# A two-layer transformer on one core: the low-rank factor split of layer 0's feed-forward moves from GpSimd to ScalarE and GpSimd together

## The reference, cut to what matters

```python
def _layernorm(x, axis=-1, eps=1e-05):
    m = jnp.mean(x, axis=axis, keepdims=True)
    v = jnp.var(x, axis=axis, keepdims=True)
    return (x - m) / jnp.sqrt(v + eps)

def _matmul_lora(x, w, a, b, scale=1.0):
    out = jnp.einsum('bsd,hd->bsh', x, w)
    out = out + jnp.einsum('bsr,hr->bsh', jnp.einsum('bsd,rd->bsr', x, a), b) * scale
    return out

mod = (_silu(L0_c) @ L0_wmod).reshape(L0_c.shape[0], 6, 1, -1)
sa, ca, ga, sb, cb, gb = (mod[:, 0], mod[:, 1], mod[:, 2], mod[:, 3], mod[:, 4], mod[:, 5])
...
h = _layernorm(x, axis=-1) * (1 + cb) + sb
gate = _matmul_lora(h, gate_w, gate_a, gate_b)          # x 1024x512, w 1376x512, a 16x512, b 1376x16
up = _matmul_lora(h, up_w, up_a, up_b)
out = _matmul_lora(silu(gate) * up, down_w, down_a, down_b)   # w 512x1376, a 16x1376, b 512x16
x = x + gb * out
```

## Time and profile before

| | before |
|---|---|
| median of three runs | 1750.19 us (1748.44 to 1757.35) |
| the profiled execution | 1748.17 us |
| its span, first to last instruction | 1746.3 us |
| mean granted TensorE clock over the span | 0.978 |
| PE busy | 1653.8 us (95%) |
| DVE busy | 1172.4 us (67%) |
| ACT busy | 1043.7 us (60%) |
| POOL busy | 746.5 us (43%) |

### The profile page before, as it was taken

One profiled execution on the slowest core, in us unless ns is written; L12 is line 12 of the kernel. 1 busy time (PEld: TensorE's weight loads), 2 busy tenths in 40 slices (PEclk: granted clock), 3 DMA queues, 4 the chain that ended last, 5 costly groups with the idle time before them and its releaser, 6 DMA issues. The chain is left out here.

```text
span 1746.3 us, 28528 instructions
## 1 busy us (share of the span) xinstructions
PE 1653.8 (95%) x10107; PEld 1338.6 (77%) x10123; DVE 1172.4 (67%) x2951; ACT 1043.7 (60%) x2261; POOL 746.5 (43%) x705
## 2 busy tenths in 40 slices
PE   4899999999999999999999699999988999999897
PEld 2689989999999989999988488878764555555476
DVE  5667677777777677777666843336777777776285
ACT  3477777877777777877777221114324666666553
POOL 3287585675856757567551300000352334321200
PEclk9999999999999999999999889999979999999998
DMA  6100100101011010000002312200230000000000
GB/s 195 38 14 22 28 25 19 32 13 38 13 31 25 20 37 13 25 19 26 13 19 79 101 40 69 67 2 19 84 82 14 1 1 1 1 1 1 1 19 31
DMA packets 75014, 55.82 MB, mean 32 GB/s; under 512 B 23502, under 2 KB 57998, under 8 KB 74874
## 3 DMA queue, kind: packets, MB, share of 16 engines
q1 hardware_dynamic: 73290, 53.21, 10.4%
q10 hardware_dynamic: 1584, 0.79, 0.2%
HBM read 51.88 MB, written 2.10 MB: 31 GB/s over the span
## 5 line engine op out<-in xcount | busy, mean ns | idle before, releaser
L792 PEld LDWEIGHTS psum<-a_probsT,a_v 128*128 128x128 f32 x2304 | 294.7, 191 | 25.6 <-issue 3.9
L792 PE MATMUL psum<-a_probsT,a_v 128*128 128x128 f32 x2304 | 299.2, 275 | 1.7 <-ACT a_probsT L1004 1.6
L893 DVE CUSTOM_DVE_ANT_0 psum<-psum,a_keys_allowed 128x128 f32<-128x128 f32 (+7 forms) x256 | 195.7, 764 | 83.0 <-PE psum L78 74.4
L2123 ACT ACTIVATE a_probsT<-psum 128x512 f32<-128x512 f32 (+1 forms) x304 | 168.4, 588 | 106.3 <-PE psum L1990 67.6
L987 ACT ACTIVATE a_probs<-psum,a_neg_max 128x128 f32<-128x128 f32 (+7 forms) x256 | 190.7, 745 | 66.6 <-DVE a_neg_max L893 58.2
L996 ACT ACTIVATE a_probs<-a_probs,a_row_inv 128x128 f32<-128x128 f32 (+7 forms) x256 | 201.1, 786 | 27.9 <-DVE a_row_inv L900 27.7
L649 POOL TENSOR_TENSOR a_turned_pool<-a_q_sum,a_sine 64x512 f32<-64x512 f32 x62 | 79.3, 1278 | 286.7 <-DVE a_q_sum L879 285.5
L923 DVE TENSOR_TENSOR a_ctxT_lo<-psum,a_ctxT_hi 128x128 fp32r<-128x128 f32 x256 | 73.7, 288 | 172.7 <-ACT a_ctxT_hi L1010 172.6
L1004 ACT COPY a_probsT<-psum 128x512 f32<-128x512 f32 (+3 forms) x384 | 173.2, 488 | 18.7 <-PE psum L780 16.6
L913 DVE SCALAR_TENSOR_TENSOR a_sumT<-psum,a_scale_o,a_sumT 128x512 f32<-128x512 f32 x248 | 173.6, 742 | 0.9 <-PE psum L806 0.7
L780 PE MATMUL psum<-ident,a_probs 128*128 128x128 f32 x1152 | 168.9, 274 | 0.5 <-ACT a_vT L981 0.3
(11 more groups left out here) (395 smaller groups left out, 3893.2 us busy)
## 6 DMA issues: line engine op xcount, KB each, us to landing
a_raw_o<-in_L_attn_qw_o SPq DMA_DIRECT2D x32, 256.0 KB, 2.8
a_raw_q<-in_L_attn_qw_q SPq DMA_DIRECT2D x31, 256.0 KB, 3.5
mod1b_w<-in_L_wmod SPq DMA_DIRECT2D x4, 1024.0 KB, 5.9
mod0a_w<-in_L_wmod SPq DMA_DIRECT2D x3, 1024.0 KB, 13.0
mod0b_w<-in_L_wmod SPq DMA_DIRECT2D x3, 1024.0 KB, 5.2
f_raw<-in_L_ffn_down_w SPq DMA_DIRECT2D x10, 256.0 KB, 3.0
f_raw<-in_L_ffn_gate_w SPq DMA_DIRECT2D x10, 256.0 KB, 3.3
f_raw<-in_L_ffn_up_w SPq DMA_DIRECT2D x10, 256.0 KB, 3.6
```

Source lines behind the costliest of these rows:

```text
L792: last = nc.tensor.matmul(bank(use)[:, 0:P], v[:, g % 2, j, :], probsT[:, u % 2, j, :], start=(j == 0), stop=(j == i))
L893: nc.vector.tensor_tensor_reduce(out=scores, in0=scores, in1=keys_allowed[:, S - (i + 1) * P:S], scale=-1.0, scalar=-MASKED, op0=ALU.add, ...
L2123: nc.scalar.activation(probsT[:, s % SLOTS, hs[0]:hs[-1] + 1, first:HALF], scores_of(group, n, HALF - first), ACT.Exp).then_inc(exped.sem, 1)
```

## The change

The factor tile `raw_b` (the short-row factors: rows of 16 numbers of `gate_b` and `up_b`) gets its place already in the attention block. POOL clears its last tile's padding after its last rotation there, and SP sends its four loads between two loads of modulation weights. In the layer norm block POOL clears, and then waits; ACT makes the six copies (`high_factors`), after its first square root and before the transposed pieces; POOL makes the four subtractions (`low_factors`) once all six copies are there. ACT's second square root now stands after the first two transposed pieces. The transposes of `down_b_stack` and ACT's copy to `down_bT` stand at the end of the layer norm block in place of the start of the feed-forward block. The new hook `"middle"` of the VectorE stream is not used by any caller.

```diff
@@ layernorm_phase, tensor and scalar streams
             if next_columns:
                 modulation.wait_columns(pe, pair)
                 next_columns.make_columns(pe, (0, 1))
+            if first_weight and "tensor" in first_weight:
+                first_weight["tensor"](pe)
...
-            for half in range(NHALF):
+            def deviation(half):
                 t_of = slice(half * TPH, (half + 1) * TPH)
                 act.wait_ge(*y_done.after(counted, half + 1))
                 nc.scalar.activation(std[:, t_of], y[:, t_of], ACT.Sqrt).then_inc(root_done.sem, 1)
+
+            deviation(0)
+            if early:
+                first_weight["between"](act)
+            else:
+                deviation(1)
...
             for i, (half, k) in enumerate(pieces):
                 act.wait_ge(*turned.after(counted, i + 1))
+                if early and i == 2:
+                    deviation(1)
                 if i >= 4:
                     act.wait_ge(*lo_done.after(counted, i - 3))
@@ layer0_attention_phase
+        early.raw_b = nc.alloc_sbuf_tensor_at("f0_raw_b", [P, NF, 2, RANK0], F32, offset=nc.sbuf_base + (-nc.sbuf_base) % 32)
+        early.low_in = mem.semaphores.enter_context(nc.semaphore("f0_low_in"))
...
             sp.wait_ge(*pool_roped.of((("q", LAST_HEAD, 1), "cosine")))
             early.load(sp, 3)
+            sp.wait_ge(*drawn.of("padding"))
+            load_up_factors(sp, w_ffn, early.raw_b, early.low_in)
             sp.wait_ge(*wo_made.of(LAST_HEAD))
             early.load(sp, 5)
...
+            pool.memset(early.raw_b[:, NF - 1, :, :], 0.0).then_inc(drawn.sem, 1)
...
+def load_up_factors(sp, w, raw_b, low_in):
+
+    last = raw_b.shape[1] - 1
+    full_rows = last * P
+    for m, name in enumerate(("gate", "up")):
+        sp.dma_start(raw_b[:, 0:last, m, :],
+                     w[name + "_b"][0:full_rows, :].rearrange("(f p) r -> p f r", p=P)).then_inc(low_in, 16)
+        sp.dma_start(raw_b[0:HID_LAST, last, m, :], w[name + "_b"][full_rows:HID, :]).then_inc(low_in, 16)
@@ layer0_ffn_phase
-        RAW_ZEROED, ZEROED, HI_STACKED, STACKED, HIDDEN_CLEARED = 3, 6, 12, 16, 17
+        RAW_ZEROED, ZEROED, HI_STACKED, STACKED, HIDDEN_CLEARED = 2, 4, 10, 14, 15
...
             sp.wait_ge(low_step, RAW_ZEROED)
-            for m, name in enumerate(("gate", "up")):
-                sp.dma_start(raw_b[:, 0:LAST, m, :],
-                             w[name + "_b"][0:FULL_ROWS, :].rearrange("(f p) r -> p f r", p=P)).then_inc(low_in, 16)
-                sp.dma_start(raw_b[0:HID_LAST, LAST, m, :], w[name + "_b"][FULL_ROWS:HID, :]).then_inc(low_in, 16)
...
-        def stack_low(pool):
+        def clear_low(pool):
...
-            pool.wait_ge(low_step, ZEROED)
-            pool.wait_ge(low_in, 16 * LOW_LOADS)
...
-            for source, stack, zeros_like in sources:
+            low_factors(pool, pool)
+
+        def high_factors(act):
+
+            act.wait_ge(low_step, ZEROED)
+            act.wait_ge(low_in, 16 * LOW_LOADS)
+            for source, stack in ((raw_b[:, :, :, :], b_stack), (raw_down_b[:, :, :], down_b_stack)):
                 for columns in (HI, ALSO_HI):
-                    pool.tensor_tensor(pick(stack, columns).bitcast(F32R), source, zeros_like, ALU.add).then_inc(low_step, 1)
-            for source, out in ((flat_raw_a, flat_a), (raw_down_a[:, :], down_a[:, :])):
-                pool.tensor_tensor(out, source, zeros(source), ALU.add).then_inc(low_step, 1)
-            pool.wait_ge(low_step, HI_STACKED)
...
+                    nc.scalar.copy(pick(stack, columns).bitcast(F32R), source).then_inc(low_step, 1)
+            nc.scalar.copy(low_a[:, :, :], raw_a[:, :, :]).then_inc(low_step, 1)
+            nc.scalar.copy(down_a[:, :], raw_down_a[:, :]).then_inc(low_step, 1)
+
+        def low_factors(engine, compute):
+
+            engine.wait_ge(low_step, HI_STACKED)
+            for source, stack in ((raw_b[:, :, :, :], b_stack), (raw_down_b[:, :, :], down_b_stack)):
+                compute.tensor_tensor(pick(stack, LO), source, pick(stack, HI), ALU.subtract).then_inc(low_step, 1)
+            for n, (source, out) in enumerate(((raw_a, low_a), (raw_down_a, down_a))):
+                engine.wait_ge(low_step, HI_STACKED + 2 + n)
+                compute.tensor_tensor(out[ALSO_HI], source[ALSO_HI], out[ALSO_HI].bitcast(F32), ALU.subtract).then_inc(low_step, 1)
...
+        def turn_down_b(pe):
+            pe.wait_ge(low_step, STACKED)
+            for k in kts:
+                last = nc.tensor.transpose(small_bank[:STACK, k * P:(k + 1) * P], down_b_stack[:, k, :], mem.ident[:, :])
+            last.then_inc(down_bT_turned, 1)
+
+        def take_down_b(act):
+            act.wait_ge(down_bT_turned, 1)
+            nc.scalar.copy(down_bT[:, :], small_bank[:STACK, :]).then_inc(down_bT_out, 1)
...
-            layernorm_phase(nc, mem, 1, loads_of_next, modulation, {"gpsimd": stack_low, "scalar": lambda act: None},
+            layernorm_phase(nc, mem, 1, loads_of_next, modulation, {"gpsimd": clear_low, "between": high_factors, "scalar": take_down_b,
+                             "tensor": turn_down_b},
                             next_modulation)
```

## The result

The changed kernel takes **1755.79 us** (median of 22 runs, 1749.05 to 1760.28) against 1750.36 (22 runs, 1746.75 to 1757.35) of the kernel before, run beside it: 1.0028 times the time, 95% interval 1.0018 to 1.0037. The forecast was 1749.8 with a range of 1744 to 1755. The change is slower by 0.3% (5.4 us by the medians), and the prediction was wrong in the size and in the reason for it.

A forecast was written before the change was run, and what follows sets the result against it. PE bounds the kernel, waiting 9.45 us for DVE in the layer norm block. Start +0.1 and `down_b_stack` -0.45 sum to -0.35 us: profiled 1748.17 becomes 1747.8, median 1749.8 (no change), range 1744 to 1755.

The forecast's parts named there:

- beyond it PE's chain through the feed-forward is the same and carries the shift to the end: After the layer norm block, PE's feed-forward work stays unchanged, so the -0.35 us sum reaches the kernel's end.
- Copies on ACT: Layer norm block: ACT's six copies take 3.3 us, bounds 3.1 to 3.9, ending at 989.55.
- rival C: Layer norm block: ACT's copies head the chain, short rows taking twice the time; 5.2 us of copies, 1751.7; chance 0.11.
- The second estimate given there: ACT's six copies by the Trainium skill's cost rule: 3.9 - 0.5 = 3.4 us, everything below 0.1 later.
- The subtractions and the lock: POOL's four subtractions take 7.1 us; they lock DVE's Newton product until 993.6, its successor until 996.8, nothing after.
- PE's wait: Between gate row and second-half transposes, PE waits for DVE's normalised tiles: within 1 us of 9.5, against 9.45 before.
- `down_b_stack`: End of layer norm block: `b_stack` transposes start 2.3 us behind the columns' end against 2.9; gain taken as 0.45 us.
- The early loads at no cost in the attention: Four factor loads moved into the attention's load queue cost zero there; without that cover, 2.20 us.
- rival D: Attention: the moved loads disturb it, making the kernel 2.2 us later, 1752; chance 0.03.
- Rival A: Layer norm block: DVE slips through POOL's lock earlier; gain at best 2.9 us there, 1746.9 in all; chance 0.12.
- B: PE keeps its full clock through second-half transposes and columns: 9 to 12 us gained, 1739 to 1741; chance 0.04.
- Rival C's addition: On top of slow copies, columns lack their stretch at clock 1.00: 11.6 us in place of 10.55, kernel 1752.8.

The follow-up runs named there:

- E11: Kernel before with only the move of `down_b_stack`'s transposes and copy to the end of the layer norm block: 1750.24 us, 1.0006 of before.
- E9: Kernel before with only the four early factor loads in the attention, POOL keeping all copies and subtractions: 1755.99 us, 1.0034 of before.
- E4: Kernel before plus 18 unused products (36 instructions) on PE behind the gate row, where it waits for DVE: 1754.47 us, 1.0021 of before.
- E12: Kernel before plus nine unused products (18 instructions) on PE behind the gate row: 1751.84 us, 1.0009 of before.
- E1: Changed kernel plus a 32-byte padding tile in place of the dropped tile of zeros: 1751.48 us, 1.0008 of before.
- E8: Changed kernel with second square root ahead of the copies, `wT` moved by 32 bytes and four unused products on PE: 1745.28 us, 0.9976 of before.
- E2: Changed kernel with `down_b_stack`'s transposes and copy back at the start of the feed-forward block: 1755.73 us, 1.0025 of before.
- E5: Kernel before with `wT` moved by 32 bytes, off a multiple of 64: 1753.27 us, 1.0021 of before.
- E10: Kernel before with only ACT's six copies and the moved square root, `wT` aligned: 1755.62 us, 1.0038 of before.
- E6: Changed kernel with `wT` alone moved by 32 bytes, back to a multiple of 64: 1752.79 us, 1.0013 of before.
- E7: Changed kernel with the second square root ahead of the copies and `wT` back at a multiple of 64: 1748.36 us, 0.9992 of before.
- E3: Changed kernel with ACT's second square root ahead of its six copies: 1751.28 us, 1.0004 of before.

## Why the prediction was wrong, point by point

- **The step that failed** is "beyond it PE's chain through the feed-forward is the same and carries the shift to the end". The instructions are the same, but a dropped tile of 32 bytes moved PE's stationary operand off a multiple of 64 bytes, and the chain got 3.0 us longer (2 to 4 by time), more than half of the 5.4. The whole diff has the line `zero = place_low(...)` go (the parts shown above leave it out); I had counted only the instructions that used it. None of the rivals had a mechanism of this kind.
- **Copies on ACT**: forecast 3.3 us, measured 3.35. Right, and the doubling for short rows in rival C did not come. (The second estimate given there adds up to 3.8 - 0.5 = 3.3 us, not 3.4.)
- **The subtractions and the lock**: forecast 7.1 us, measured 6.8 (991.06 to 997.83). The lock caught L298, one step later than forecast: L300 starts 0.07 us behind POOL's end, and only it, not two steps, lies ahead of the normalisations. PE's wait: forecast 9.5, measured 9.01.
- **`down_b_stack`**: forecast 2.3 us behind the columns, measured 2.44, and E11 shows that it can't be timed.
- **The early loads at no cost in the attention**: on average the block starts as early with them as without (977.4 against 977.2), so rival D's 2.2 us are not there. Single profiles differ by more (978.8 in E9), which stays open.
- **Rival A** (1746.9): its condition came true, its price did not. The product's successor (L296) did get in ahead of POOL's longest subtraction, but the next step (L298) was caught. With the block's later start of 1.53 us taken out, the first normalisation started at 996.57, where A had "996.8, or less" and the forecast 997.2, and PE at 998.53, 0.5 us earlier than before and not 2.9. **B** did not happen; E4 and E12 show that a filled wait doesn't bring it either, since the columns lose the clock again.
- **Rival C's addition** ("the 1.00 stretch inside the columns does not come") did happen in the profiled execution. Its price was too low: 64 x 0.18 = 11.6 us forecast, 13.65 measured. The 0.18 came from 11 products counted in a stretch of 2 us, and the count takes in those that the stretch's edges cut; from start to start it is 0.213, in before too. By the same count B's 0.1 at 1.00 is 0.112 from start to start.
- **The range** treated the clock as noise around one execution. Over the runs the time follows the mean granted clock: profiled executions of before, E1 and E8 at 0.978 took 1748.0 to 1748.7 us, those of after, E2, E5 and E9 at 0.970 to 0.973 took 1756.4 to 1759.3. Which clock an execution gets changes with the kernel: 0.973 or less came in 8 of the 104 runs of before beside the experiments, in 12 of 22 of after, 8 of 10 of E9, 8 of 12 of E10, 4 of 11 of E1, 5 of 12 of E6, 1 of 12 of E7 and none of E8 or E11. The kernels in which PE waits longest ahead of the columns (E9 and E10) have it most often: 2.1 us more of waiting in E9, 6.8 of time. That the wait is what does it is not shown.

**What stays open.** With `wT` in place the change has a stage 0.9 us shorter in the profiles of E1 and E6 (38.2 us from block start to `b_stack`, against 39.0), but a median that is 1.4 and 3.2 us longer. More of its executions have a lower clock (the counts above); the profiles don't show why, and the intervals reach no difference. The clock's fall between the eleventh `hidden` and the casts with an unaligned `wT` isn't explained either.

## What to carry to other kernels

A tile that a change adds or drops moves every address behind it: work out the start of the operands that the dominant loop reads before and after, and keep them, with padding if need be. When small work goes from one engine to another, look at what stood first in the receiver's queue: here a square root of 0.20 us put behind 3.35 us of copies was worth 3 to 4 us. And a part of a change is not worth the same alone: loads and copies each cost 6 us, and together a fraction of it.

## What the runs showed of the hardware

- **Placement of a stationary operand.** With `wT` starting 32 bytes off a multiple of 64, ten tiles with some 48 products of 512 columns each took 137.5 us and not 136.1, at a granted clock of 1.00. The weight loads show the same mean (188 ns) in both; the step from product to product is 235.9 ns on average (235.2 in E5) where it was 232.8. Starts at 202272 and 202336 were slow, one at 202304 was not; other distances weren't tried, and which part of PE's reading pays isn't shown.
- **Products with a moving side of one column** took 0.213 us each at 0.50 (13.65 / 64) and 0.112 at 1.00 (the middle 30 in before). PE counted as busy through all of them, but the clock rose and fell again during them in before, fell in E4 and E12, and stayed at 0.50 in E8, where PE had been busy for most of the wait ahead of them.
- **A lock costs a small instruction the whole of the other's**: 2.94 us for a step of 128x4 (0.17 when free) beside a subtraction of 3.08, 3.31 for the cast of E3 (0.42 when free) beside one of 3.42.
- **ACT's copies of 64-byte pieces** took no more than long rows: two of 352 elements in 0.87 us.
